# Exponentials of score blocks in attention: one 128x2048 instruction for two of 128x1024

## What is computed

```python
def reference(x, Wq, Wk, Wv, w, W1, b1, W2, b2):
    xn = layernorm(x)                                  # eps 1e-5
    q, k, v = heads(xn @ Wq.T), heads(xn @ Wk.T), heads(xn @ Wv.T)   # 16 heads of 64
    attn = einsum('bqhd,bkhd->bhqk', q, k) / 8
    attn = attn * mask                                 # 1 inside a group, sigmoid(w) outside
    s = softmax(attn) @ v
    h = relu(xn @ ternary(W1).T + b1)                  # 4096 wide
    g = silu(h @ ternary(W2).T + b2)
    return x + s * g
```

## Time and profile before

| | us |
|---|---|
| two runs | 1442.89 and 1519.28 |
| their median | 1481.09 |
| the profiled execution | 1443.67 |
| span of its slowest core, core 4 | 1441.8 |
| spans of its 8 cores | 1434.6 to 1441.8 |

### The profile page before, as it was taken

How to read it: one execution, slowest core, us unless ns; L and a number is a source line. 1 busy time by engine, 2 the same in 40 slices (tenths; PEclk the granted TensorE clock), 3 DMA queues, 4 the chain that set the end, 5 groups by cost and what they waited for, 6 DMA issues and landing times.

```text
span 1441.8 us, 16189 instructions; the slowest of 8 cores (1434.6 to 1441.8 us)
## 1 busy us (share of the span) xinstructions
PE 1116.7 (77%) x4923; PEld 441.1 (31%) x4986; DVE 517.8 (36%) x469; ACT 709.1 (49%) x729; POOL 43.5 (3%) x87
## 2 busy tenths in 40 slices
PE   2659788878787877776777759989989979984563
PEld 0124333323232322222222214434434434431221
DVE  2490132323323232222122264346164253513554
ACT  0213478786868799998999952201200210221110
POOL 0000000000000000000000000000000000000000
PEclk9999999999999999999999989999999999996775
DMA  9641001010101021111122244313041340403331
GB/s 223 127 59 59 30 30 59 30 59 30 60 30 59 30 88 59 50 49 50 59 59 59 60 116 118 75 43 108 13 114 37 81 117 1 118 0 117 117 117 59
DMA packets 25129, 99.83 MB, mean 69 GB/s; under 512 B 4554, under 2 KB 4554, under 8 KB 19930
## 3 DMA queue, kind: packets, MB, share of 16 engines
q1 hardware_dynamic: 18474, 83.91, 19.7%
q0 software_dynamic: 6576, 14.88, 4.6%
HBM read 96.49 MB, written 8.39 MB: 73 GB/s over the span
## 4 chain that ended last, share of the span: by engine, by line
PE 46%; ACT 26%; issue 11%; DVE 9%; DMA 6%; ACTq 0%; SPq 0%; DVEq 0%; POOL 0%; POOLq 0%
ACT arena L645 25%; PE PS L867 15%; PE PS L902 10%; PE PS L439 7%; PE PS L664 4%; DMA arena<-arena 4%; PE PS L369 4%; PE PS L601 2%; DMA arena<-xT 2%; DVE arena L574 2%; DVE arena L571 1%; DVE arena L842 1%; DVE arena L836 1%; DVE arena L827 1%; PE PS L392 1%
## 5 line engine op out<-in xcount | busy, mean ns | idle before, releaser
L645 ACT ACTIVATE arena<-PS,arena 128x1024 bf16<-128x1024 f32 (+1 forms) x640 | 596.7, 1086 | 104.5 <-PE PS L606 104.1
L601 PE MATMUL PS<-arena 64*128 64x512 bf16 x512 | 190.4, 383 | 146.3 <-ACT arena L645 142.9
L664 PE MATMUL PS<-arena 128*65 128x512 bf16 x1024 | 273.9, 390 | 1.6 <-ACT arena L645 0.7
L902 PE MATMUL PS<-arena 128*128 128x512 bf16 x1003 | 241.6, 402 | 27.1 <-ACT arena L878 9.7
L878 ACT ACTIVATE arena<-PS,arena 128x2048 bf16<-128x2048 f32 x32 | 63.0, 1968 | 351.5 <-PE PS L867 351.5
L867 PE MATMUL PS<-arena 128*128 128x512 bf16 x1003 | 222.2, 381 | 11.4 <-DVE arena L712 10.4
L606 PE MATMUL PS<-arena 64*128 64x512 bf16 x512 | 194.5, 391 | 0.0
L902 PEld LDWEIGHTS PS<-arena 128*128 128x128 bf16 x1024 | 104.1, 103 | 167.1 <-issue 61.2
L601 PEld LDWEIGHTS PS<-arena 64*128 64x128 bf16 x512 | 45.1, 93 | 314.9 <-issue 314.8
L867 PEld LDWEIGHTS PS<-arena 128*128 128x128 bf16 x1024 | 100.6, 98 | 132.5 <-issue 13.2
L709 DVE CAST arena<-PS 64x512 bf16<-64x512 f32 x64 | 43.7, 683 | 248.5 <-PE PS L664 247.5
(11 more groups left out here) (69 smaller groups left out, 437.9 us busy)
## 6 DMA issues: line engine op xcount, KB each, us to landing
arena<-xT SPq DMA_DIRECT2D x16, 1024.0 KB, 10.8
arena<-w1T SPq DMA_DIRECT2D x16, 1024.0 KB, 6.0
arena<-w2T SPq DMA_DIRECT2D x16, 1024.0 KB, 6.1
arena<-w1T SPq DMA_DIRECT2D x32, 512.0 KB, 5.3
arena<-w2T SPq DMA_DIRECT2D x32, 512.0 KB, 4.8
outT<-arena POOLq DMA_DIRECT2D x8, 1024.0 KB, 8.4
arena<-wvT POOLq DMA_DIRECT2D x1, 2048.0 KB, 36.6
arena<-wkT POOLq DMA_DIRECT2D x1, 2048.0 KB, 18.4
```

The costliest lines, as they stand in the source:

```text
L601: b.opn("pe", lambda t, kc=kc, pbase=pbase, hp=hp, qs=qs: t.matmul(PS[:, pbase:pbase + 512], sb["kb"][0:64, hp * T + kc * 128:hp * T + (kc ...
L645: t_exp[gi] = b.op("act", lambda a, inap=inap, outap=outap, sc_t=sc_t: a.activation(out=outap, in_=inap, func=AF.Exp, scale=sc_t[:, 0:1], ...
L664: tpv = emit("pe", lambda t, kc=kc, hh=hh, slot=slot, hp=hp, abase=abase: t.matmul(PS[0:65, abase + hh * 512:abase + (hh + 1) * 512], sb[" ...
L902: tok_ = emit("pe", lambda t, dc=dc, ts=ts, fc=fc, base=base: t.matmul(PS[:, base + ts * 512:base + (ts + 1) * 512], sb["w2q"][:, fc * D + ...
```

## The change

Where both key chunks of a pair have one scale for the whole query slice, one call of `emit_exp_merged` takes the place of two calls of `emit_exp`. This is so for 6 of the 8 pairs of a pass, so 192 instructions of 128x2048 stand where 384 of 128x1024 stood; the 256 half instructions stay.

```diff
         for kc0 in range(0, KC, 2):
             emit_scores(itp, kc0)
             emit_scores(itp, kc0 + 1)
-            emit_exp(itp, kc0)
-            emit_exp(itp, kc0 + 1)
+            ilo0, ihi0 = kc_mask(itp, kc0)
+            ilo1, ihi1 = kc_mask(itp, kc0 + 1)
+            if ihi0 <= ilo0 and ihi1 <= ilo1:
+                emit_exp_merged(itp, kc0)
+            else:
+                emit_exp(itp, kc0)
+                emit_exp(itp, kc0 + 1)
```

## The result

The changed kernel takes 1581.8 us (median), the kernel before beside it 1443.1. The ratio is 1.0958 with a 95% interval of 1.0946 to 1.0971: slower by 139 us. The forecast was 1581 for an execution like the profiled one. In some executions of either kernel, the one of 1519.28 us before among them, the cores of a die show a lower granted clock and take longer; the ratio leaves these out.

What follows compares the result with a forecast made beforehand. ScalarE was taken to bound plain passes, TensorE's order the end of woven ones. 93 us (plain) + 46 (woven) - 2 (ends) = +137 on the profiled 1443.67 gave 1581 us, range 1550 to 1640.

Steps and rivals of the forecast that it cites:

- What bounds the kernel: Attention: ScalarE limits passes without projection blocks, busy 111.50 of 111.60 us; with blocks, TensorE's order limits the pass end.
- Duration: ScalarE in attention: one merged exponential of 128x2048 takes 2.06 us, from a full one's 1.21 plus 0.85.
- Gap: Between two merged exponentials ScalarE idles 0.92 us: 0.14 hand-over, 0.23 second chunk's scores, 0.55 until ScalarE starts.
- the seams: Where split and merged pairs meet: +0.80 us for a split pair behind a merged one, +0.56 the other way.
- Plain passes: The 18 attention passes without projection blocks: 5.2 us more a pass, +93 us in all.
- The term for the ends: Last attention pass: one or two steps hidden behind VectorE's quantizing, started from the threshold at `kc0 = 8`: -1.6 us.
- Woven passes: The 14 attention passes with projection blocks on TensorE: five of eight steps exposed, 3.3 us a pass, +46 us.
- The three hidden steps: Steps at the two projection blocks of a pass: nothing behind each block, +0.1 us at most from `kc0 = 8` to 10.
- The clock's case: Rival, chance 0.15: TensorE's clock falls too in attention, gap 1.31 us, +31 to +60 us more, taken as 1622.
- The case of the merge that pays: Rival, chance 0.03: on full ScalarE two exponentials of 1.10 us become one of 1.95, faster, 1406 us.

Runs made afterwards that it cites:

- the added matmuls: The changed kernel with four more matmuls of 512 columns, which nothing waits for, behind the weighted sums of chosen pairs: 1576.7 us, ratio 1.0928.
- the run with buffers of its own: Kernel before, without weighted sums and evacuations in passes 15 to 22, scores using 4096 PSUM columns, merging in 19 to 22: unmerged passes 18.4 us, merged 17.0.

## Why the prediction was right

*What bounds the kernel.* Right: full in plain passes, ScalarE left nothing to hide an idle of its own, and every 0.91 us came through to the end. One reading was loose: in the slices ScalarE stands at 6 to 9 tenths from the sixth to the twenty-third, not at 7 to 9 from the fifth to the twenty-fourth. Nothing was worked out from it.

*Duration.* 2.06 us forecast, 2.057 measured, from one full exponential plus 1024 elements; L883 keeps its 1.97, so taking the nearest width would have been 0.09 short.

*Gap.* 0.92 forecast, 0.91 in 85 of the 94 steps from merged to merged in plain passes of core 6; four more stand at 1.33, at the lower clock. At the seams 0.69, as forecast.

*Plain passes.* A pass was to grow by 5.2 us and grew from 18.5 to 23.8 on average in the sixteen without thresholds, by the starts of their first exponentials. The part grew by 89.5 us for 93 less 2. The term for the ends was too small: both passes with thresholds, 23 and 31, grew by only about 3 us, which is 4 us less where 1.6 had been taken off. ScalarE had waited there before: 0.43, 0.51 and 0.14 us in front of three pairs of pass 23, 2.28 and 0.51 in front of two of pass 31, and these waits cover part of the new ones.

*Woven passes.* 46 us forecast, 49 measured. The three hidden steps are seen one by one in pass 8 of the changed kernel: the step from `kc0` = 8 to 10 grew by 0.77 us, the one behind the first block shrank by 0.67, which leaves 0.10 as forecast, and the one behind the second block grew by nothing. The run with merges only behind the blocks, at 0 us, confirms the last two. The 3 us over are the clock's. Of core 6's woven passes, 4, 5, 12 and 13 hold a stretch of 3.4 us at the lower level and core 1's same passes hold none; they take 28.52, 29.31, 28.53 and 29.62 us on core 6 and 28.09, 27.92, 28.09 and 28.14 on core 1, 3.7 us more in all. With the added matmuls the woven part took 390.8 to 391.6 us on the eight cores, about 46 over before.

*The rivals.* The clock's case had its price right, 1.31 us of gap forecast and 1.33 measured, and its frequency wrong by far: few steps of the 160, 5 us in all instead of 31 to 60. The Trainium skill's rule on groups of matmuls that cycle through PSUM ("TensorE: Matmul & The Clock Gate", section on psum-queue depth-cycling) agrees with the trace in kind, as the clock fell 9 to 11 times on a core where it had fallen twice. The case of the merge that pays was refuted here by the gap of 0.91 us and confirmed where the buffers allow it, with 0.22 us for each merge. The Trainium skill's advice to group operations on a saturated engine ("Perfetto Trace Analysis", section on optimizing Scalar/DVE operations) agrees with the run with buffers of its own and not with the changed kernel, and its 51 ns are small against the 0.22 us measured.

Errors of opposite sign, the clock's +5 and the thresholds' passes' -3, help the sum to lie within 1 us of the measured median. The terms are right to some 4 us each and no better.

## What to carry to other kernels

Before merging two instructions on a full engine, look at what their operands' buffers do between them: if the two halves are each other's double buffer, the merge saves one instruction's fixed cost (0.24 us here, 0.13 of it left where each instruction starts from idle) and pays the whole round trip to the producer (0.91 us). Price it at each step from one group to the next, because it is free where something else holds the next group up anyway. Then look for a grouping along another axis, here scale instead of chunk, that saves instructions and leaves the buffers alone.

## What the runs showed of the hardware that was not expected

TensorE's clock fell to its lower level without any long pause: in the 6.8 us before the fall at 672.4 us it was busy for 3.50 us, and its longest idle was the 1.37 us before the scores at 672.57, in which the fall lies. Matmuls that nobody needs, put into TensorE's idle time, took 14 us off one kernel and 5 off another. And at the lower level, where it stayed for 150 us on end in the run with buffers of its own, TensorE still kept a full ScalarE supplied over the 106 us shown, once the scores had all 4096 columns and the weighted sums were left out.
